# Edge sums of a two-layer graph network: the turned flags compared directly from rows of edge ends

## What is computed

```
# layer 0, one head (layer 1: the same with 8 heads of 32 columns)
xp    = xn @ W.T                          # 3125 x 256
e     = leaky_relu(a_src[src] + a_dst[dst], 0.2)
ex    = exp(e - segment_max(e, dst))      # per edge
denom = segment_sum(ex, dst)
agg   = segment_sum((ex / denom[dst])[:, None] * xp[src], dst)
```

## Time and profile before

| | |
|---|---|
| median of 3 runs | 1892.24 us (1891.11 to 1894.18) |
| span of the profiled execution | 2276.6 us |
| one-head edge stage in it, first gather to end | about 67 to 742 us |
| eight-head edge stage in it | about 1176 to 1930 us |
| busy over the whole span | PE 1646.4, DVE 1163.6, ACT 656.1, POOL 1009.6 us |

### The profile page before, as it was taken

The page is one execution under the profiler, slowest core; times in us unless marked ns, Lnnn a source line. Parts: engine busy times, 40 slices in busy tenths (PEclk is TensorE's granted clock), DMA queues, the critical chain, the costliest instruction groups (busy, mean ns, idle before and its releaser), DMA issues. The chain is left out here.

```text
span 2276.6 us, 34460 instructions
## 1 busy us (share of the span) xinstructions
PE 1646.4 (72%) x9468; PEld 1342.0 (59%) x9468; DVE 1163.6 (51%) x3309; ACT 656.1 (29%) x2160; POOL 1009.6 (44%) x1093
## 2 busy tenths in 40 slices
PE   5177776677778978999463665777577777689991
PEld 4045555556656557999343554555455556689991
DVE  7256566555456664222452555556566657841223
ACT  4222121122322554333152222332222212643330
POOL 4556555656543002555124545555454541325550
PEclk9588888889889989999786777888787989599996
DMA  7323222333222016666532222222222220267666
GB/s 167 98 71 84 80 75 75 87 82 87 78 70 58 1 63 224 211 213 210 135 112 72 80 74 77 74 80 75 70 77 68 72 72 20 93 199 213 215 202 178
DMA packets 148002, 244.24 MB, mean 107 GB/s; under 512 B 53369, under 2 KB 83368, under 8 KB 147558
## 3 DMA queue, kind: packets, MB, share of 16 engines
q0 software_dynamic: 48384, 134.19, 21.1%
q1 hardware_dynamic: 97306, 106.27, 15.7%
q10 hardware_dynamic: 2124, 1.54, 0.3%
HBM read 210.48 MB, written 31.21 MB: 106 GB/s over the span
## 5 line engine op out<-in xcount | busy, mean ns | idle before, releaser
L679 POOL DMA_INDIRECT es_rows<-table,eall x784 | 745.7, 951 | 719.3 <-SPq L668 418.6
L699 PE MATMUL bank<-es_msg,es_one 128*125 128x264 f32 x976 | 305.3, 466 | 123.5 <-DVE es_msg L822 104.1
L699 PE MATMUL bank<-es_rows,es_won 128*125 x976 | 289.8, 448 | 116.8 <-DVE es_won L819 84.8
L762 ACT ACTIVATE es_oneT<-bank 125x512 bf16<-125x512 f32 x244 | 145.1, 595 | 755.9 <-remote 488.5
L699 PEld LDWEIGHTS bank<-es_msg,es_one 128*125 128x125 f32 x976 | 209.0, 225 | 175.2 <-DVE es_msg L822 113.9
L699 PEld LDWEIGHTS bank<-es_rows,es_won 128*125 128x125 f32 x976 | 202.4, 218 | 159.2 <-issue 125.3
L842 DVE TENSOR_TENSOR es_z<-es_rows,es_near 128x4 f32<-128x4 f32 (+1 forms) x244 | 43.1, 177 | 359.3 <-ACTq L774 265.2
L1237 PE MATMUL bank<-ffn_xbT,ffn_w 128*128 128x128 f32 x1792 | 220.8, 277 | 0.0
L1290 ACT ACTIVATE xT<-bank,ffn_b1s 128x128 f32<-128x128 f32 x448 | 128.2, 369 | 303.2 <-PE bank L1237 292.6
L1396 DVE TENSOR_TENSOR xT<-bank,xT 128x256 f32<-128x256 f32 x112 | 47.6, 425 | 327.8 <-issue 190.1
L1247 PE MATMUL bank<-ffn_w,xT 128*128 x896 | 211.7, 379 | 0.0
(11 more groups left out here) (445 smaller groups left out, 2408.8 us busy)
## 6 DMA issues: line engine op xcount, KB each, us to landing
ffn_w<-in_L_ffn_W SPq DMA_DIRECT2D x112, 512.0 KB
es_rows<-table,eall POOLq DMA_INDIRECT x784
ffn_w<-yrows SPq DMA_DIRECT2D x20, 560.0 KB
ffn_w<-in_L_ffn_W SPq DMA_DIRECT2D x2, 4096.0 KB
xrows<-acc SPq DMA_DIRECT2D x10, 560.0 KB
table<-acc SPq DMA_DIRECT2D x5, 577.5 KB
table<-acc SPq DMA_DIRECT2D x5, 564.4 KB
out_x<-xs SPq DMA_DIRECT2D x5, 560.0 KB
```

The lines of the kernel that those rows point to most:

```text
L679: pool.indirect_dma_start(rows[:, q % R, w, :], None, m.table[H], bass.IndirectOffsetOnAxis(ap=m.eall[:, at:at + 1], axis=0)).then_inc(gat ...
L699: ins = pe.matmul(sum_banks[p % 2][0:P, 0:W], left, right, start=(w == 0), stop=(w == BW - 1))
L762: a.activation(oneT[:, p % 2, :], turn_bank[0:P, :], ACT.Copy).then_inc(kept, 1)
```

## The change

**Own ends as rows.** A new DRAM array `ends_rows` holds the own end of each of the 50,176 places as 16-bit integers in the order of the list. The one-head stage makes it in front of its loop: four transposes on PE of `m.ends`, one copy on ACT to 16 bits, four stores by SP, and a wait for them. SP then loads two blocks at a time, the same row to all 125 partitions (125 x 1024 values of 2 bytes), 49 loads in each stage, into `near_end`; `landed` also waits for them.

**Flags.** `flags(i+1)` on VectorE is one compare of such a row (125 x 512, 16-bit) with the node number of each partition (`m.node_of`), and writes `oneT` in bf16. `turn` on PE, the copy of the turned flags on ACT and the bf16 identity are gone.

**Order of a step.** `scores(i)` follows in the same iteration, `sums` is for i-2, the scores' four operations and `weigh` for i-1, `add` for i-3. One signal, `answered`, is given after PE's `sums(i-2)` and `scores(i)`, ahead of the mixing block's products; DVE waits for it once, at the head of the iteration. Score products go to two banks in turn. ACT lays the score pieces first (`lay(i+1)`), and its `landed` and `ready` are for block i, at the end.

**One head.** `mark` is gone; `weigh` is four operations, each (node numbers == own end) x weight for 128 x 125, with two operands read per partition (`m.ends` and `wts`, both in SBUF now). A buffer is freed when the step is `added`. **Eight heads.** `mark` stays, for step i-1 between the reduce and the four operations.

The diff, cut to what is spoken of:

```diff
-    R, O = 8, 5
+    R = 8
...
-        one = sb("_one", [128, O, BW, P], BF16 if H == 1 else F32)
+        near_end = sb("_near_end", [P, R, BLOCK], I16)
...
             won = sb("_won", [128, 2, BW, P])
+            wts = sb("_wts", [128, 2, BW, H])
+            turned_ends = sb("_turned_ends", [QUARTER, 4, 128], I16)
         else:
+            one = sb("_one", [128, 2, BW, P])
             msg = sb("_msg", [128, 2, BW, D + H])
-        ident = sb("_ident", [128, 128], BF16)
+            wts = m.bank[6][:, NBLK * BW:NBLK * BW + 2 * BW * H].rearrange("p (s w h) -> p s w h", s=2, w=BW)
+            ends = m.bank[6][:, 0:NBLK * BW]
...
-        scores_of = [m.bank[1][:, i * BW * 6 * H:(i + 1) * BW * 6 * H].rearrange("p (w x) -> p w x", w=BW) for i in (0, 1)]
+        sum_banks = m.bank[2:4]
+        scores_of = [m.bank[i][:, 0:BW * 6 * H].rearrange("p (w x) -> p w x", w=BW) for i in (0, 1)]
...
-                done = summed if H == 1 else weighed
+                done = added if H == 1 else weighed
                 last_of = column(sp, DONE, STEPS, checked=True)
+
+                def load_ends(k):
+                    lo, hi = k * CHUNK, min((k + 1) * CHUNK, NBLK)
+                    at = k % BUFS * CHUNK
+                    sp.dma_start(near_end[:, at:at + hi - lo, :].rearrange("p q e -> p (q e)"),
+                                 m.ends_rows[lo * BLOCK:hi * BLOCK].partition_broadcast(P)).then_inc(ends_in[k % BUFS], 16)
+
+                if H == 1:
+                    sp.wait_ge(ends_kept, 1)
+                    for j in range(4):
+                        sp.dma_start(m.ends_rows[j * QUARTER * 128:(j + 1) * QUARTER * 128].rearrange("(r n) -> r n", n=128),
+                                     turned_ends[:, j, :]).then_inc(ends_stored, 16)
+                    sp.wait_ge(ends_stored, 64)
+                for k in range(BUFS):
+                    load_ends(k)
                 for q in range(NBLK):
                     last = last_of(q - LATE) if 0 <= q - LATE < NBLK - R else None
                     sp.wait_ge(gathered[q % R], (q // R + 1) * (16 * BW))
+                    for k in (0, 1) if q == 0 else [(q + 2) // CHUNK] if q % CHUNK == 0 and q + 2 < NBLK else ():
+                        sp.wait_ge(ends_in[k % BUFS], 16 * (k // BUFS + 1))
                     sp.sem_inc(landed, 1)
                     if last is not None:
                         sp.wait_ge(done, last)
                         sp.sem_inc(freed, 1)
+                        if (q - LATE) % CHUNK == CHUNK - 1 and (q - LATE) // CHUNK + BUFS < NCHUNK:
+                            load_ends((q - LATE) // CHUNK + BUFS)
...
+                if H == 1:
+                    for j in range(4):
+                        ins = pe.transpose(m.bank[0][0:QUARTER, j * 128:(j + 1) * 128], m.ends[:, j * QUARTER:(j + 1) * QUARTER], m.ident[:, :])
+                    ins.then_inc(ends_turned, 1)
+                    pe.wait_ge(ends_kept, 1)
...
                 def scores(p):
-                    pe.wait_ge(kept, p + 1)
-                    if p >= 1:
-                        pe.wait_ge(zchain, 4 * p - 3)
+                    pe.wait_ge(flagged, p + 1)
+                    pe.wait_ge(staged, p + 1)
+                    if p >= 2:
+                        pe.wait_ge(zchain, 4 * (p - 2) + 1)
                     for w in range(BW):
                         ins = pe.matmul(scores_of[p % 2][:, w, :], oneT[:, p % 2, w * 128:(w + 1) * 128],
                                         stage[:, p % 4, :], start=True, stop=True)
-                    ins.then_inc(scored, 1)
-
-                def turn(p):
-                    pe.wait_ge(marked, p + 1)
-                    if p >= 1:
...
-                    ins.then_inc(turned, 1)
-
-                for i in range(STEPS + 4):
-                    if valid(i - 4):
-                        sums(i - 4)
+                    return ins
+
+                for i in range(STEPS + 2):
                     if valid(i - 2):
-                        scores(i - 2)
+                        ins = sums(i - 2)
+                    if valid(i):
+                        ins = scores(i)
+                    ins.then_inc(answered, 1)
                     side.tensor(pe, i)
-                    if valid(i):
...
                 if H == 1:
+                    a.wait_ge(ends_turned, 1)
+                    a.activation(turned_ends[:, :, :].rearrange("r j n -> r (j n)"), m.bank[0][0:QUARTER, :], ACT.Copy).then_inc(ends_kept, 1)
...
-                def keep(p):
+                def lay(p):
                     tile = tile_of(p)
                     if p >= 4:
-                        a.wait_ge(scored, p - 3)
-                    a.activation(stage[:, p % 4, :], row_of(parts, tile), ACT.Copy)
...
-                        a.wait_ge(scored, p - 1)
-                    a.activation(oneT[:, p % 2, :], turn_bank[0:P, :], ACT.Copy).then_inc(kept, 1)
...
-                for i in range(STEPS + 4):
+                        a.wait_ge(answered, p - 3)
...
+                lay(0)
+                for i in range(STEPS + 2):
...
+                    if valid(i + 1):
+                        lay(i + 1)
                     side.scalar(a, i)
-                    if valid(i - 3):
-                        expose(i - 3)
+                    if valid(i - 1):
+                        expose(i - 1)
                     if valid(i):
-                        keep(i)
-                    if valid(i - 2):
-                        a.wait_ge(landed, block_of(i - 2) + 1)
+                        a.wait_ge(landed, block_of(i) + 1)
                         a.sem_inc(ready, 1)
...
-                    v.wait_ge(summed, p + 1)
...
+                def flags(p):
+                    block_ends = near_end[:, bass.ds(slot_of(p), 1), :].rearrange("p a e -> p (a e)")
+                    v.tensor_scalar(oneT[:, p % 2, :], block_ends, m.node_of[:, bass.ds(tile_of(p), 1)], None, ALU.is_equal).then_inc(flagged, 1)
...
                     own = ends[:, bass.ds(block_of(p) * BW, BW)].unsqueeze(2).to_broadcast([128, BW, P])
-                    v.tensor_tensor(one[:, p % O, :, :], nodes, own, ALU.is_equal).then_inc(marked, 1)
+                    v.tensor_tensor(one[:, p % 2, :, :], nodes, own, ALU.is_equal)
...
-                        v.tensor_tensor(won[:, p % 2, :, :], one[:, p % O, :, :], wts[:, p % 2, :, :].to_broadcast([128, BW, P]),
-                                        ALU.mult).then_inc(weighed, 1)
+                        for w in range(BW):
+                            ins = v.tensor_scalar(won[:, p % 2, w, :], m.nodes[:, bass.ds(tile_of(p) * P, P)],
+                                                  m.ends[:, bass.ds(block_of(p) * BW + w, 1)], wts[:, p % 2, w, 0:1], ALU.is_equal, ALU.mult)
+                        ins.then_inc(weighed, 1)
...
+                v.wait_ge(ends_in[0], 16)
+                flags(0)
+                for i in range(STEPS + 3):
+                    p, p1, p3 = i, i - 1, i - 3
+                    zq, yq = z[:, p1 % 2, :, :], y[:, p1 % 2, :, :]
+                    if i >= 1:
+                        v.wait_ge(answered, i)
+                    if valid(p1):
+                        v.tensor_reduce(near[:, p1 % 2, :, :], scores_of[p1 % 2].rearrange("p w (c x) -> p w x c", c=3),
+                                        AX.X, ALU.add).then_inc(zchain, 1)
+                        if H > 1:
+                            mark(p1)
+                        here = rows_of(p1, D, D + H)
+                        v.wait_ge(ready, p1 + 1)
+                        v.wait_ge(zchain, 4 * p1 + 1)
+                        if H > 1 and p1 >= 2:
+                            v.wait_ge(laid, p1 - 1)
+                        v.tensor_tensor(zq, here, near[:, p1 % 2, :, 0:H], ALU.add).then_inc(zchain, 1)
+                        v.wait_ge(zchain, 4 * p1 + 2)
+                        v.scalar_tensor_tensor(yq, zq, SLOPE, zq, ALU.mult, ALU.max).then_inc(zchain, 1)
+                        v.wait_ge(zchain, 4 * p1 + 3)
+                        v.tensor_tensor(zq, yq, near[:, p1 % 2, :, H:2 * H], ALU.subtract).then_inc(zchain, 1)
+                        v.wait_ge(zchain, 4 * p1 + 4)
+                        v.tensor_scalar(zq, zq, 0.0, None, ALU.min).then_inc(zed, 1)
...
+                    if valid(i + 1):
+                        flags(i + 1)
...
                     if valid(p3):
-                        v.wait_ge(scored, p3 + 1)
-                        v.tensor_reduce(near[:, p3 % 2, :, :], scores_of[p3 % 2].rearrange("p w (c x) -> p w x c", c=3),
-                                        AX.X, ALU.add).then_inc(zchain, 1)
-                    if valid(p):
...
-                    for of, p, turn in ((tile_of, i + 3, 5), (block_of, i + 2, 6), (slot_of, i - 1, 1)):
+                    if valid(p1):
+                        weigh(p1)
+                    for of, p, turn in ((tile_of, i + 3, 5), (slot_of, i + 2, 6), (block_of, i + 1, 7)):
...
```

(54 more changed lines are left out.)

51 lines of the change are left out of this document (6 added, 45 removed).

## The result

| | before | after |
|---|---|---|
| median | 1891.67 us (4 runs) | 1857.72 us (4 runs, 1855.68 to 1861.94) |
| profiled execution: own time, span | span 2276.6 us | own time 1861.94, span 1860.2 us |

The ratio is 0.9821 (95% interval 0.9802 to 0.9841): 34 us less. The forecast was 1876, 16 us less. The time lies just inside the range (1857 to 1906) and on the forecast side, but the gain is twice the one forecast, and much of it comes from a stage that the forecast had at nothing.

The account below looks back on a forecast made before the run. Gathers were taken to bound both edge stages, except the eight-head stage's last third, bound by the loop. Terms -27 + 10 + 1 - 1 = -17 took 1892 to 1875, stated as 1876 us; range 1857 to 1906.

Parts of the forecast that it names:

- Gathers against steps, and the stretched profile: Both edge stages: gathers produce, steps consume; the profiled execution, 384.4 us above the median, was taken to stretch little else.
- Where the 40 us lie: Time above the gather pace, some 40 us, placed in the last third of the eight-head stage, where the loop bounds.
- pairs: Two steps in Mix1's output part, eight-head stage: 9.42 us before with register loads, 8.23 forecast after the change.
- the hold: VectorE operations with all operands in SBUF delay gathers: +10 us in the one-head stage, +1 in the eight-head stage.
- The mechanism: Mix1's output part: DVE's L842 waits 1.34 us for ACT's signal, which follows the end of PE's long iteration.
- nothing, covered by the gathers: One-head stage: DVE's +0.1 us a step and the work removed from PE and ACT change nothing behind the gathers.
- PE's 0.40 us a step: One-head stage, if gathers were no cover and PE bound the loop: a gain of at most 49 us.
- Flags: The new VectorE compare, 125 x 512 in 16 bits: 0.49 us, in line about 0.41, lower bound 0.27.
- The rival with cheap flags: Flags at 0.27 us and no hold on gathers: -34 us and -2 elsewhere, 1858 us; chance 0.17.
- Loads, prelude, new single wait: Loads hidden, one-head prelude 0, at most +3 us; a late prelude or single-wait bound shared a last 0.05 chance.

Follow-up runs that it names:

- the clean traces: Unstretched traces: the kernel before, run again with no edit (1895.1 us), and the changed kernel (own time 1861.94 us).
- experiment 5: The kernel before with ScalarE's checked register load of the blocks moved to the head of its iteration: 1894.9 us, ratio 1.002.
- experiment 2: Each kernel with one gather instead of four per block from the ninth block on: 1877.0 us for the kernel before, 1799.0 us for the changed one.
- the move alone: The kernel before with TensorE's turn put first, ahead of the mixing block's products, in both stages: 1852.1 us, ratio 0.978.
- a_again: The changed kernel, unchanged, as a control on another chip: 1857.9 us.
- the old weights: The changed kernel with the one-head weights as before (compare and product, ends and weights in PSUM): 1852.3 us; 1854.8 us on another chip.
- b_again: The kernel before, run again with no edit for a trace that is not stretched: 1895.1 us in one execution.

## Why the prediction was right and wrong

- *Gathers against steps, and the stretched profile.* Right: the clean traces have 855 us around the stages, taken as 848 with stages that end some 3 us later each, and the gatherers' pace is the floor of the one-head stage and of the other up to about step 66.
- *Where the 40 us lie.* **This step failed.** "With 502 for the one-head stage that is 1046, against 1044 left for them. The model fits": the sum fitted with two errors in it. The eight-head stage had 523 us, 526 to the end that the prediction used, not 544: loads were added to pairs that hid them (experiment 5), 0.6 us over 23 pairs, 14 us; the rest is in the last steps. The one-head stage had 515, or 518, instead of 502 and was bound by its loop throughout (experiment 2). The forecast had the one-head stage 9 us longer after the change (+10 for the hold) and the eight-head stage 26 shorter; the clean traces have 12 and 21 shorter. A pair of numbers that must add up to a known total doesn't test how they share it.
- *The mechanism.* Right, and its price in Mix1's part nearly: DVE's wait for a signal from the end of TensorE's iteration. It held in Mix0's keys too, where no stretch of the trace was read for it. The term "nothing, covered by the gathers" is what failed most: 12 us there, 21 with the move alone. Nor was it PE's 0.40 us a step, the gain that the prediction named in case the gathers were no cover: the move alone takes nothing off PE.
- *Flags.* Taken at 0.41 us in line, measured 0.27, the lower bound: 47 x 0.14 = 6.6 us more gain. The stage's gain was still forecast 5 us too large, since its base had 14 us of loads that weren't there. 512 wide and 16 bits it lasts 353 ns, as long as the 256-wide f32 row. By the Trainium skill, VectorE: DVE Perf Modes, "Mode 4×_2P — both tricks at once", such an operation gives four elements per cycle; the trace agrees in so far as twice the elements take the time of that f32 row. The pair was forecast at 8.23 and is 7.85; VectorE is its bound, as forecast.
- *The hold.* Right in sign, too large: 10 us taken. What L838 and `flags` hold adds up to 3.1 us in `a_again`; between first and last gather the difference is 2 to 6 us (497.5 and 495.1 against 491.4 and 492.6 with the old weights, 491.1 with turn first). L838 was priced as a full hold of 0.2 us and gives 0.05. The Trainium skill, SBUF — State Buffer, "SBUF: two separate sides", lets a VectorE operation in a mode with both ports, or one with two SBUF inputs against a GpSimd one that reads SBUF, and the GpSimd one exclude each other for the whole instruction. L1885, with two SBUF inputs, holds a gather to its end less 0.13; an L838 of 0.34 could by that hold 0.21 and holds 0.13 at most, so for it the rule shows only in part.
- *The rival with cheap flags* named 1858, and its own terms, -34 and -2, give 1856. It had flags right and the gatherers' hold and the one-head stage wrong, so that the number came out is luck. So is the time's place in the range: its lower end came from this rival, not from the one-head stage.
- *Loads, prelude, new single wait.* 0 each; no row contradicts it: outside the stages there are 855 us before and after, and no gather waits for `freed`.

The 5.8 us by which the version with turn first beats the change aren't explained in full. In the traces its one-head stage is 6.8 us shorter than in `a_again`, 4 of them between first and last gather, which may be the hold, and its eight-head stage 2.8 us longer.

## What to carry to other kernels

Where an engine works for a main loop and for side work in one iteration, give the signal for which others wait before the side work: here one moved call gave 41.6 us, while a rewrite of the data path gave 34. Ask of each stage by itself who paces it; a run with most of the transfers left out answers that in one trace. When the profiled execution is far longer than the runs, take another before building on it.

## What the runs showed that I had not expected

- With three quarters of the gathers of all but eight blocks gone the kernel before became only 18 us faster.
- TensorE's idle of 3.34 us was followed by 10 us at a mean granted clock of 0.53, in which Mix0's products took 3.75 us instead of 1.96. There a late signal was paid twice. As a cause of the gain it counts little: from 67 to 600 us, with the whole one-head stage in it, the mean clock is 0.91 in `b_again` and 0.92 with turn first, and the changed kernel has such stretches too.

```profile
67.00:600.00 533.00, 435.02 (x2623) 341.58 (x2624) 375.61 (x1200) 159.16 (x466) 373.44 (x392) 0.91 0.37 98
```

```profile
67.00:600.00 533.00, 448.11 (x2718) 350.40 (x2719) 392.59 (x1241) 172.43 (x505) 372.91 (x392) 0.92 0.37 99
```

- The 0.35 us operation added to a full VectorE cost 32 us over 122 steps, some 25 of them from step 66 on.
